# Retention output group: eight state matmuls, then eight value matmuls, in one PSUM bank

## The reference, cut to what matters

```python
state = gb * state + jnp.einsum('bhi,bhj->bhij', v_t, k_t)      # per token, per head
y_t = jnp.einsum('bhij,bhj->bhi', state, q_t)
...
y = y @ out_w.T + out_b
x = layernorm(x + y)
h = silu(x @ w1.T * s1) * (x @ w2.T * s2)          # hidden width 4096
h = gelu(h @ h1.T * s1h);  h = gelu(h @ h2.T * s2h)
x = layernorm(x + h @ w3.T * s3)
```

## Time and profile before

| | us |
|---|---|
| median of 3 runs | 2854.01 |
| lowest and highest of them | 2841.47, 3107.86 |
| the profiled execution | 2842.7 |
| span of its slowest core (core 3) | 2841.2 |
| spans of its eight cores | 2837.6 to 2841.2 |
| granted TensorE clock, as a share of full speed | 0.992 to 0.993 |

### The profile page before, as it was taken

The page is one execution under the profiler, slowest core; times in us unless marked ns, Lnnn a source line. Parts: engine busy times, 40 slices in busy tenths (PEclk is TensorE's granted clock), DMA queues, the critical chain, the costliest instruction groups (busy, mean ns, idle before and its releaser), DMA issues.

```text
span 2841.2 us, 31537 instructions; the slowest of 8 cores (2837.6 to 2841.2 us)
## 1 busy us (share of the span) xinstructions
PE 2769.3 (97%) x13568; PEld 1259.3 (44%) x13568; DVE 380.4 (13%) x562; ACT 431.1 (15%) x627; POOL 128.2 (5%) x243
## 2 busy tenths in 40 slices
PE   5799999999999999999999999999999999999997
PEld 2344444444444444444444444444444444444443
DVE  3355653200000000000001143100000000000004
ACT  2232333110010010001000232100100010010011
POOL 1000000000000000000000000000000000000000
PEclk9899999999999999999999999999999999999998
DMA  9935344464444444444444355644444444444441
GB/s 172 166 72 108 68 75 75 74 100 79 79 77 75 74 75 78 78 80 77 75 75 67 62 101 105 97 79 79 78 76 75 74 76 78 78 79 76 75 75 60
DMA packets 47784, 235.73 MB, mean 83 GB/s; under 512 B 4896, under 2 KB 9120, under 8 KB 26016
## 3 DMA queue, kind: packets, MB, share of 16 engines
q0 software_dynamic: 38000, 216.02, 47.8%
q1 hardware_dynamic: 9648, 17.69, 2.1%
HBM read 441.31 MB, written 8.39 MB: 158 GB/s over the span
## 4 chain that ended last, share of the span: by engine, by line
PE 96%; DMA 3%; issue 0%; DVE 0%; ACT 0%; POOL 0%; DVEq 0%; ACTq 0%; POOLq 0%
PE PS L375 70%; PE PS L365 16%; PE PS L337 3%; PE PS L343 2%; DMA PB<-wvr 2%; PE PS L352 2%; PE PS L357 1%; DMA PB<-wqk 1%; PE PS L414 1%; PE PS L411 1%; PE PS L385 0%; PE PS L397 0%; PE PS L426 0%; ACT X1T L668 0%; DVE R L524 0%
## 5 line engine op out<-in xcount | busy, mean ns | idle before, releaser
L375 PE MATMUL PS<-R,PB 128*128 128x512 bf16 x8960 | 1934.4, 379 | 0.0
L375 PEld LDWEIGHTS PS<-R,PB 128*128 128x128 bf16 x8960 | 876.8, 98 | 1057.1
L365 PE MATMUL PS<-X1T,PB 128*128 128x512 bf16 x2048 | 444.9, 379 | 0.0
L661 ACT ACTIVATE R<-PS,CFS 128x512 bf16<-128x512 f32 x256 | 175.9, 687 | 1577.1 <-PE PS L375 1577.0
L365 PEld LDWEIGHTS PS<-X1T,PB 128*128 128x128 bf16 x2048 | 199.6, 98 | 239.7
L510 DVE SCALAR_TENSOR_TENSOR R<-PS,CFS,X1T 128x512 f32<-128x512 f32 x32 | 24.0, 751 | 1959.5 <-PE PS L375 1959.5
L337 PE MATMUL PS<-X1T,PB 128*128 128x512 bf16 x512 | 120.2, 389 | 26.7 <-DMA PB<-wqk 26.7
L505 DVE SCALAR_TENSOR_TENSOR R<-PS,CFS,TMPA 128x512 bf16<-128x512 f32 x128 | 96.1, 751 | 295.0 <-PE PS L365 274.9
L653 ACT ACTIVATE TMPA<-PS,CFS 128x512 f32<-128x512 f32 x128 | 87.7, 687 | 315.1 <-PE PS L365 315.0
L337 PEld LDWEIGHTS PS<-X1T,PB 128*128 128x128 bf16 x512 | 48.6, 99 | 85.7 <-issue 33.3
L343 PE MATMUL PS<-PB,X1T 128*128 128x512 bf16 x256 | 60.9, 394 | 17.1 <-DMA PB<-wvr 17.1
(11 more groups left out here) (63 smaller groups left out, 563.2 us busy)
## 6 DMA issues: line engine op xcount, KB each, us to landing
PB<-h1p POOLq DMA_DIRECT2D x64, 1024.0 KB, 9.9
PB<-h2p POOLq DMA_DIRECT2D x64, 1024.0 KB, 9.9
PB<-w POOLq DMA_DIRECT2D x64, 512.0 KB, 5.7
PB<-wqk POOLq DMA_DIRECT2D x15, 1024.0 KB, 25.0
PB<-w3p POOLq DMA_DIRECT2D x12, 1024.0 KB, 9.8
R<-xT SPq DMA_DIRECT2D x32, 256.0 KB, 7.3
PB<-wvr POOLq DMA_DIRECT2D x8, 1024.0 KB, 15.7
yT<-R SPq DMA_DIRECT2D x32, 256.0 KB, 3.0
```

Source lines behind the costliest of these rows:

```text
L365: mm = t.matmul(bank, PB[panels_of(tl)[0] % 4][:, o:o + 128], xs(2 * tb + th, c), start=(c == 0), stop=(c == 7))
L375: mm = t.matmul(bank, pb[:, c * 128:c * 128 + 128], h1b(c, th) if kind == "h2" else ub(c, th), start=(c == 0), stop=(c == 31))
L661: s.activation(h1b(ot, th) if kind == "h1" else ub(ot, th), bank, AF.Gelu, scale=cf("s1h" if kind == "h1" else "s2h", ot, 1)).then_inc(don ...
```

## The change

Inside `yout` the loop over the four head pairs is split into two loops: first the eight state matmuls of the group, then its eight value matmuls. The number, the operands, the places in the array and the shapes of the matmuls stay; the waits ahead and the count behind stay.

What changes with the order is how the bank is opened. Before, each state matmul carried `start=True`, which overwrites and begins a new sum. Now only the first of them in each half of the partitions (`i == 0`) carries it, and the six others go without it: they write to columns in which nothing has been written since, and the value matmuls add to them.

```diff
                     pr = 4 * g + i
                     for p0 in (0, 64):
                         t.matmul(YB[p0:p0 + 64, i * 128:i * 128 + 128], sbt(c)[p0:p0 + 64, pr * 64:pr * 64 + 64],
-                                 qtil(c, pr * 128, 128)[p0:p0 + 64, :], start=True, stop=False, tile_position=(p0, p0))
+                                 qtil(c, pr * 128, 128)[p0:p0 + 64, :], start=(i == 0), stop=False,
+                                 tile_position=(p0, p0), skip_group_check=True)
+                for i in range(4):
+                    pr = 4 * g + i
                     for p0 in (0, 64):
                         mm = t.matmul(YB[p0:p0 + 64, i * 128:i * 128 + 128], vw(w, cl, pr * 128 + p0, 64),
                                       amat(g, (p0 // 64 * 4 + i) * 128, 128), start=False, stop=True,
-                                      tile_position=(0, p0))
+                                      tile_position=(0, p0), skip_group_check=True)
                 mm.then_inc(p_y, 1)
```

## The result

| | before | after |
|---|---|---|
| median of 13 runs, us | 2854.78 | 2823.35 |
| lowest run, us | 2841.21 | 2822.31 |
| the profiled execution, us | 2842.7 | 2822.33 |
| spans of its eight cores, us | 2837.6 to 2841.2 | 2818.2 to 2820.8 |

The ratio of after to before is 0.9931, with a 95% interval of 0.9911 to 0.9952: the time fell by 0.7%, which is clear of the noise but under the 2% that would count as faster. The forecast was 2824.2 us and no change beyond 2%.

What follows compares the result with a forecast made beforehand. TensorE, busy 97% of the span, was taken to bound the kernel. 27 groups x 0.705 us = 19.0, less 0.5 for new waits, took 18.5 from 2842.7: 2824.2 us, range 2813 to 2845, within 2% of no change.

Steps and rivals of the forecast that it cites:

- The price of a step: In the `yout` group, six of eight steps out of a shape (0.175 us) become inner steps (0.0575 us), saving 0.705 us.
- the reading of `kvout`: From `kvout`'s eight pairs in 0.37 us: 0.175 us for the step out, seven inner steps of 0.028 us, taken as shortest.
- the low end's 23.8 us: Gain over all counted groups if inner steps took 0.028 us; used for the range's low end of 2813 us.
- 27 groups, not 32: Five groups precede the second transfer's arrival at 133 us; their 3.5 us go into transfer waits, leaving 19.0 us.
- The new waits: TensorE waits for VectorE's bank releases at two tiles around window 3's layer norm: about 0.2 us each, 0.5 with hand-over.
- The sum: Over the whole execution: 19.0 us saved in the groups less 0.5 us of new waits, 18.5 us.
- The clock: Shifts can add or remove clock falls behind TensorE's waits: 1.7 us each, at most two either way, no likely sign.
- No side-by-side work: Rival: the two matmuls of a state pair run serially, inner step 0.115 us, gain 13.8 us, 2829 us; chance 0.07.
- A price of the pair: Rival: small-weight pairs in the group cost 0.175 us whatever follows, so nothing changes, 2843 us; chance 0.07.
- A wait for the sum: Rival: value pairs wait for columns their state pair just wrote; gain up to 21.7 us, 2821 us; chance 0.04.
- Slower blocks: Rival: weight loads into the same cells wait for the running pair, step 0.34 us, 27 us slower, 2869 us; chance 0.02.
- The execution: The range's high end, 2845 us, allowed 11.3 us for a median execution of the whole kernel instead of the profiled one.

Runs made afterwards that it cites:

- Kernels 2 to 4: The group of before reordered, with new start flags: value pairs lagging by one, 2836.97 us; two head pairs at a time, 2828.01; shape change after every matmul, 2888.98.
- Kernel 7: New order in the first five groups only, old order with new start flags in the 27 others, against before: lowest run 2841.43 us, ratio 0.9997.
- Kernels 9, 10 and 11: Changed kernel with `kvout` behind the value block and block-diagonal state, 2823.47 us; that with state casts last, 2817.43; changed kernel with layer norm preparation before two evacuations, 2818.69.
- kernel 4: State and value matmuls alternating singly, so the shape changes after every matmul, against before: lower of two runs 2888.98 us, group 2.749 us.
- kernel 6: Changed kernel without the four state matmuls at (64, 64): one execution, 2842.92 us; its two cores at 0.99 of the clock have spans of 2821.5 and 2820.5 us.
- kernel 2: New start flags and value pairs lagging one behind their state pairs, six steps out of a shape, against before: lowest run 2836.97 us, ratio 0.9999.
- kernel 10: Changed kernel with `kvout` behind the value block, block-diagonal state weights, and ScalarE's state casts behind the last layer norm preparation: lowest run 2817.43 us, ratio to before 0.9923.

## Why the prediction was right, point by point

- **The price of a step.** The forecast took 0.175 us for a step out of a shape and 0.0575 for one inside, 0.705 us saved a group. Measured 0.715. The inner steps of the 64x64 block, for which the trace of before had no row, are those of the value block. The step out is 0.149 to 0.155 us behind a longer block, and the three inner ones are 0.080, 0.056 and 0.056: a block's inner steps were put 0.02 us too low and its step out 0.02 us or more too high. That these two errors cancel is luck. The same error stands in the reading of `kvout`: its single starts show inner steps of 0.053 and then 0.031 to 0.032 us and a step out of 0.132, so 0.028 was not the shortest step, and the low end's 23.8 us were some 0.5 too many. Kernels 2 to 4 show that it is the change of shape that costs.
- **27 groups, not 32.** Over the eight cores the first tile behind the second transfer starts at a median of 132.1 us before and 132.2 after, while the five groups ahead of it are each 0.715 us shorter. Kernel 7 shows it alone. The list of waits of the slowest cores shows less of it (43.8 us before, 45.2 after) because these are different cores, and the arrival differs by 2 us between cores. Over all eight the sum of the last two waits went from a median of 14.2 to 17.0 us, 2.8 more where 3.5 were forecast.
- **The new waits.** Both are there, at the tiles and with the sizes that the forecast gave. The timeline of TensorE after, with the two tiles and the scores ahead of the second, and VectorE's evacuation that frees its bank:

```profile
353.85 1.89 PE L365 MATMUL PS<-X1T,PB 128*128 128x512 bf16 x8 [0.22 <-DVE R L508]
...
366.66 0.40 PE L385 MATMUL PS<-R 64*128 64x128 bf16 x8
367.17 3.61 PE L365 MATMUL PS<-X1T,PB 128*128 128x512 bf16 x16
```
```profile
366.28 1.40 DVE L508 SCALAR_TENSOR_TENSOR R<-PS,CFS,TMPA 128x512 bf16<-128x512 f32 x2
```

  The second is in no list of waits, because the scores' modelled end hides most of it. But the scores hold the array for 0.51 us here and for 0.33 at the same place of before (385.01 to 385.34), and the tile starts just behind the 367.02 at which the first evacuation ends: a wait of 0.18 us, the same on all eight cores. The 0.5 us put for both were 0.4.

- **The sum.** 27 x 0.715 - 0.4 = 18.9 us; 18.5 was forecast. The medians over the cores' spans went from 2839.2 to 2819.5 us, 19.7 us, and the profiled executions differ by 20.4 us. The next point tells of the 0.8 us between 18.9 and 19.7. The part behind the last group kept its length, as forecast: a median of 2445.8 us before and 2445.6 after.
- **The clock.** Behind the waits of 1.94 us a fall moved: core 3 of before had it at 277 us, core 2 of after has it at 191, and in both kernels it comes in three of the 16 places. There it had no part in the result, as assumed. Behind the second transfer it probably had one, of about 1 us: from that tile to the next `scores(c, 0)`, with one group between, 6.8 to 9.0 us pass before (median 9.0) and 5.7 to 7.1 after (median 6.7), more than the group's 0.7 us; from 133 to 155 us core 1 was granted 0.81 before and 0.89 after. That is inside the 3.4 us by which the forecast widened its range. The forecast treated the falls as chance alone. Kernels 9, 10 and 11 show that they hang on the wait: at 3.2 us they came in 16 of 16 places, at 1.94 us in 3 of 16, at 0.6 us in none of 12; kernel 4 has falls without any wait.
- **The rivals.** No side-by-side work: excluded by kernel 6. A price of the pair: excluded by the change itself, whose pairs step at 0.056 us, and by kernel 4. A wait for the sum: excluded by kernel 2. Slower blocks: the inner steps are 0.056 to 0.080 us.
- **The execution.** The high end of the range allowed 11.3 us for a median execution in place of the profiled one. The median of after is 2823.35 us, 1.0 us over its profiled execution, so the allowance was not needed.

## What to carry to other kernels

Count the changes of matmul shape (rows by columns of the weight) along TensorE's program and order small matmuls so that equal shapes are neighbours: each change avoided between small matmuls saved 0.12 us here. Four head pairs shared a bank here, with only the first matmul of each partition half opening it. Before counting a saving, mark which of the places lie ahead of a wait for a transfer behind fully busy DMA engines; those gave nothing here. When an edit shortens TensorE's program, look at the in-order engine that feeds its next wait: exchanging two lines on ScalarE was worth 6.0 us, more than the 4.9 us by which kernel 10, with both shape edits, is under the changed kernel.

## What the runs showed of the hardware that was not expected

- A single matmul between two changes of shape holds the array as long as a pair, 0.17 us.
- Matmuls at (0, 0) and (64, 64) run at the same time even with three others between them in the program: eight in that order took 0.35 us, four of them alone 0.34 us.
- TensorE's clock can fall without a wait: with 2.75 us groups of single matmuls between dense tiles, core 1 was granted 0.86 over 25 us in which TensorE never waited, and 81 of its dense matmuls between 76 and 560 us ran at about the lower level, where core 1 of before had 19. With the wait ahead of the layer norm matmuls at 3.2 us it fell every time (16 of 16), at 1.94 us now and then (3 of 16 in each of three kernels), at 0.6 us never (12 places).
